# VectorE makes the last sum of probabilities, denominators before turned maxima, and the activations' loads placed anew

## The reference, cut to what matters

```python
# layer 0: 16 heads of 64, inner width 1024, no norm, all heads with own k, v
q, k, v = x @ Wq, ctx @ Wk, ctx @ Wv
logits  = q k^T / 8 + col_bias          # -20 * (1 - mask) in the columns of four tokens
out     = softmax(logits) v @ Wo + bo + x
# layers 1 to 3: 16 heads of 32, 4 heads of k and v, each shared by 4 query heads
xn  = x / sqrt(mean(x^2) + 1e-5) * norm_w
out = x + softmax((xn @ wq) k^T / sqrt(32)) v @ wo
```

## Time and profile before

| | us |
|---|---|
| median of 3 runs | 4437.71 (4436.86 to 4444.43) |
| profiled execution, its own time | 4435.94 |
| its span | 4434.0 |
| project_contexts | 0 to about 975 |
| a0 | about 975 to 2212 |
| a1 | about 2214 to 4434 |

### The profile page before, as it was taken

How to read it: one execution, slowest core, us unless ns; L and a number is a source line. 1 busy time by engine, 2 the same in 40 slices (tenths; PEclk the granted TensorE clock), 3 DMA queues, 4 the chain that set the end, 5 groups by cost and what they waited for, 6 DMA issues and landing times.

```text
span 4434.0 us, 62707 instructions
## 1 busy us (share of the span) xinstructions
PE 4157.8 (94%) x19560; PEld 2635.8 (59%) x19560; DVE 2582.5 (58%) x3586; ACT 2009.9 (45%) x2506; POOL 1842.3 (42%) x924
## 2 busy tenths in 40 slices
PE   9999999987999999999879999999999999999998
PEld 7888888874555555555535555554555544554555
DVE  3122200015556555655577777778777778777777
ACT  2111211114334333433346566656665666656665
POOL 0000000003445444544445566555665555656665
PEclk9999999998999999999979999999999999999999
DMA  5333422234444444444433322332233233322233
GB/s 183 131 128 137 160 85 82 95 108 114 121 124 114 123 122 117 118 124 124 113 83 94 87 72 78 93 105 68 75 88 94 74 85 94 87 85 75 84 88 102
DMA packets 321408, 458.07 MB, mean 103 GB/s; under 512 B 46184, under 2 KB 118888, under 8 KB 321352
## 3 DMA queue, kind: packets, MB, share of 16 engines
q1 hardware_dynamic: 321352, 457.32, 36.6%
HBM read 223.82 MB, written 102.77 MB: 74 GB/s over the span
## 4 chain that ended last, share of the span: by engine, by line
PE 36%; DVE 5%; ACT 5%; issue 4%; SPq 0%; ACTq 0%; DVEq 0%; POOL 0%; DMA 0%
PE a_ps L1186 7%; PE a_ps L1146 7%; PE a_ps L1211 6%; PE a_ps L1128 6%; PE a_ps L1170 6%; ACT a_probs L915 4%; DVE x_lo L1001 2%; PE a_ps L1197 1%; PE a_ps L1202 1%; DVE a_max_cols L995 1%; PE a_ps L1153 1%; PE a_ps L1116 0%; DVE a_qf L985 0%; DVE a_results L1036 0%; DVE wq_lo L962 0%
## 5 line engine op out<-in xcount | busy, mean ns | idle before, releaser
L995 DVE TENSOR_REDUCE a_max_cols<-a_ps 128x1 f32<-128x512 f32 x2086 | 1345.2, 677 | 298.9 <-PE a_ps L1146 294.7
L915 ACT ACTIVATE a_probs<-a_ps 128x1024 f32<-128x1024 f32 x1024 | 1016.5, 1026 | 668.9 <-PE a_ps L1170 653.5
L806 POOL TENSOR_TENSOR a_sums<-a_probs 128x1024 f32<-128x1024 f32 x256 | 606.5, 2384 | 815.9 <-ACT a_probs L915 815.9
L1146 PE MATMUL a_ps<-a_k_ops,a_q_ops 96*128 96x512 f32 x2086 | 822.6, 430 | 58.0 <-DVE a_max_cols L995 28.2
L1011 DVE RECIPROCAL a_stage<-a_stage 128x128 f32<-128x128 f32 x640 | 573.0, 925 | 491.9 <-ACT a_stage L891 491.9
L1170 PE MATMUL a_ps<-a_q_ops,a_k_ops 128*128 128x512 f32 x2560 | 789.6, 410 | 52.9 <-ACT a_probs L915 38.4
L806 POOL TENSOR_TENSOR a_sums<-a_sums,a_probs 128x1024 f32<-128x1024 f32 x320 | 768.4, 2412 | 20.7 <-POOL a_sums L806 12.7
L1186 PE MATMUL a_ps<-a_probs,a_v 128*32 128x512 f32 (+1 forms) x4096 | 662.8, 615 | 33.7 <-ACT a_probs L915 32.1
L1146 PEld LDWEIGHTS a_ps<-a_k_ops,a_q_ops 96*128 96x128 f32 x2086 | 387.9, 191 | 424.0 <-DVE a_max_cols L995 301.6
L1170 PEld LDWEIGHTS a_ps<-a_q_ops,a_k_ops 128*128 128x128 f32 x2560 | 451.4, 190 | 296.5 <-ACT a_probs L915 194.8
L881 ACT ACTIVATE a_q_ops<-a_ps 1x512 fp32r<-1x512 f32 x518 | 304.4, 588 | 296.0 <-PE a_ps L1153 289.5
(11 more groups left out here) (87 smaller groups left out, 5180.6 us busy)
## 6 DMA issues: line engine op xcount, KB each, us to landing
a_k_ops<-k_scratch SPq DMA_DIRECT2D x201, 256.0 KB, 3.9
a_q_ops<-a_qn_hi SPq DMA_DIRECT2D x792, 64.0 KB, 2.0
k_scratch<-cp_out SPq DMA_DIRECT2D x88, 512.0 KB, 2.8
a_q_ops<-a_qn_hi SPq DMA_DIRECT2D x268, 128.0 KB, 2.3
cp_raw<-in_ctx_t SPq DMA_DIRECT2D x64, 512.0 KB, 4.0
a_x_raw<-out_t SPq DMA_DIRECT2D x26, 1024.0 KB, 5.4
a_q_ops<-a_qn_lo SPq DMA_DIRECT2D x396, 64.0 KB, 2.0
a_x_res<-out_t SPq DMA_DIRECT2D x96, 256.0 KB, 3.3
```

What stands on the lines that cost most here:

```text
L806: pool.tensor_tensor(sums[:, hp], (probs if i == 1 else sums)[:, hp], probs[:, n], ALU.add)\
L915: act.activation(probs[:, s], ps[:, 2 * (s % 2):2 * (s % 2) + 2, :], ACT.Exp)\
L995: dve.tensor_reduce(max_cols[:, t % 2, col:col + 1], bank(max_bank(p)), AX.X, ALU.max, negate=True).then_inc(reduced, 1)
L1146: pe.matmul(bank(max_bank(p)), q_ops[0:SHIFT, s, h, PASS - 1, q * P:(q + 1) * P], k_ops[0:SHIFT, s, k_head(h), PASS - 1, :], start=True, s ...
```

## The change

In a0, for every tile:

- POOL makes two of the three sums; the third (`last_sum`) is made by DVE, behind its first six reductions and ahead of the reciprocals. It waits for POOL's second sum and for the fourth exponential.
- PE makes `denominators` before `turn` instead of behind it. ACT's order of `shift` and `take_denominators` stays.

In a0, for every batch: `load_x` is issued at the start of tile 4 instead of tile 0, and both rests of x are taken in tile 5 behind the sixth reduction, ahead of `last_sum`. In the last batch x of a1's first batch is loaded and split instead.

At the head of a0 v is loaded after q of tile 1; Wo goes through `x_raw` in two halves, of which only the first is loaded before the loop. They are split in batch 0, in tile 1 and tile 3, on ACT behind the third exponential and on DVE behind the fifth reduction. Each engine has an `If` for it, passed in every batch.

At the head of a1 load, rounding and rest of x fall away; PE sums the four squares itself (four matmuls instead of POOL's three adds and one matmul).

```diff
-    XAT = (1, 4)
+    WO_AT = (1, 3)
-    LOAD_AT = 2 if has_norm else 0
+    LOAD_AT = 2 if has_norm else T - 4
-        x_raw = sb("x_raw", [P, CK, S], F32)
+        x_raw = shared["x_raw"]
-            w_raw = probs[:, 0:4].rearrange("p (a b) c s -> p a (b c s)", a=2)
+            w_raw = x_raw[:, :, :].rearrange("p (a k) s -> p a (k s)", a=1)
...
             if has_norm:
-                load_x(0)
...
                 load_k(0, 0)
-                load_v(0)
-                for c in range(HALF):
-                    sp.dma_start(raw_chunk(HALF + c, c)[0], chunk(wo[0], HALF + c)).then_inc(w_in[c], DMA)
...
                 load_q(0, 0)
-                for t in range(1, AHEAD):
-                    load_k(0, t)
+                load_k(0, 1)
+                load_q(0, 1)
+                load_v(0)
+                load_k(0, 2)
+                load_q(0, 2)
+                sp.dma_start(raw_chunk(HALF, 0)[0], chunk(wo[0], HALF)).then_inc(w_in[0], DMA)
...
+                        if has_norm:
+                            x_free()
+                            load_x((it + 2) % B)
+                        else:
+                            with sp.If(it < N - 1):
+                                sp.wait_ge(w_split, HALF)
+                                x_free()
+                                load_x((it + 1) % B)
+                            with sp.Else():
+                                x_free()
+                                sp.dma_start(x_raw[:, :, :], x_out[0].rearrange("(k p) s -> p k s", p=P))\
+                                    .then_inc(x_in_s, DMA)
+                    if t == WO_AT[1] - 1 and not has_norm:
+                        with sp.If(it == 0):
+                            sp.wait_ge(w_split, 1)
+                            sp.dma_start(raw_chunk(HALF + 1, 0)[0], chunk(wo[0], HALF + 1)).then_inc(w_in[0], DMA)
...
             def sum_probs(it, t):
-                for i in range(1, max(PRE)):
+                for i in range(1, max(PRE) if has_norm else KT - 1):
...
-            if has_norm:
-                sum_squares(0)
...
             if has_norm:
-                round_x(0, 0)
                 squares(0)
...
-            if not has_norm:
-                for c in range(HALF):
-                    round_chunk(HALF + c, c, 1)
-                act.wait_ge(w_split, HALF)
...
+                        if not has_norm and t in WO_AT and s == NS // 2:
+                            with act.If(it == 0):
+                                round_chunk(HALF + WO_AT.index(t), 0, WO_AT.index(t) + 1)
...
             if has_norm:
-                split_x(0, 0)
                 rest_chunk(0, 0, 1)
...
             if not has_norm:
-                for c in range(HALF):
-                    rest_chunk(HALF + c, c, c + 1)
...
+            def last_sum(it, t):
+                dve.wait_ge(summed, (it * T + t) * SUMS + SUMS - 1)
+                dve.wait_ge(exped, (it * T + t + 1) * NS)
+                dve.tensor_tensor(sums[:, 0], sums[:, 0], probs[:, NS - 1], ALU.add).then_inc(summed, 1)
+
             def head_tile(it, t):
...
-                    if t == SPLIT_AT and i in XAT:
-                        split_x(it + 1, XAT.index(i))
+                    if t in WO_AT and i == M // 2:
+                        with dve.If(it == 0):
+                            rest_chunk(HALF + WO_AT.index(t), 0, WO_AT.index(t) + 1)
+                if t == SPLIT_AT:
+                    for c in range(XC):
+                        split_x(it + 1, c)
+                last_sum(it, t)
                 reciprocals(it, t, range(2))
...
-            def sum_squares(n):
+            def sum_squares(n, parts=1):
                 pe.wait_ge(sq_step, (n + 1) * SQ)
-                pe.matmul(bank(SUMB), ones[:, :], sq[:, 0, :], start=True, stop=True).then_inc(ssum_done, 1)
+                for k in range(parts):
+                    last = pe.matmul(bank(SUMB), ones[:, :], sq[:, k, :], start=(k == 0), stop=(k == parts - 1))
+                last.then_inc(ssum_done, 1)
...
                     outputs(it, t, kt)
+                denominators(it, t)
                 turn(*place(it, t + 1))
-                denominators(it, t)
                 free_q(it, t)
```

More of the change, by code:

```diff
@@ L702, in _ @@
                 load_v(0)
-                sp.wait_ge(x_split, 1)
-                sp.wait_ge(sq_step, 1)
+                sp.wait_ge(sq_step, SQ)
                 load_x(1)
@@ L708, in _ @@
                     .then_inc(w_in[0], DMA)
-            for t in range(0 if has_norm else 1, AHEAD):
-                load_q(0, t)
+                for t in range(AHEAD):
+                    load_q(0, t)
             with sp.Fori(0, N) as it:
@@ L718, in _, with x_free @@
                     if t == LOAD_AT:
-                        sp.wait_ge(x_split, (it + 1 + EARLIER) * XC)
-                        for i in range(RES):
-                            sp.wait_ge(stored[i], 1 + it * (UR * DMA))
-                        load_x((it + 1 + EARLIER) % B)
+                        def x_free():
+                            sp.wait_ge(x_split, (it + 1 + EARLIER) * XC)
+                            for i in range(RES):
+                                sp.wait_ge(stored[i], 1 + it * (UR * DMA))
+                        if has_norm:
[14 more added lines that the diff above has]
+                            sp.dma_start(raw_chunk(HALF + 1, 0)[0], chunk(wo[0], HALF + 1)).then_inc(w_in[0], DMA)
                     if t == 0 and has_norm:
@@ L778, in _ @@
             pool.sem_inc(added, CK)
-            if not has_norm:
-                pool.sem_inc(x_in_s, DMA)
-                pool.sem_inc(x_hi_done, XC)
-                pool.sem_inc(x_split, XC)
+            pool.sem_inc(x_in_s, DMA)
+            pool.sem_inc(x_hi_done, XC)
+            pool.sem_inc(x_split, XC)
+            if has_norm:
+                pool.sem_inc(sq_step, CK - 1)
             pool.memset(ident[:, :], 0.0).then_inc(consts, 1)
@@ L1112, in _ @@
             bank_q = q_taken if has_norm else q_lo
-            def sum_squares(n):
+            def sum_squares(n, parts=1):
                 pe.wait_ge(sq_step, (n + 1) * SQ)
-                pe.matmul(bank(SUMB), ones[:, :], sq[:, 0, :], start=True, stop=True).then_inc(ssum_done, 1)
+                for k in range(parts):
+                    last = pe.matmul(bank(SUMB), ones[:, :], sq[:, k, :], start=(k == 0), stop=(k == parts - 1))
+                last.then_inc(ssum_done, 1)
             def project_q(it, t, tiles=range(CK), first=False, early=False):
                 if t == 0 and 0 in tiles and has_norm:
-                    pe.wait_ge(ms_step, MS * it + 1)
                     if not first:
@@ L1218, in _ @@
                 pe.wait_ge(consts_v, 4)
-                sum_squares(0)
+                sum_squares(0, CK)
                 pe.wait_ge(w_split, 1)
             for t in range(AHEAD):
+                if has_norm and t == AHEAD - 1:
+                    pe.wait_ge(ms_step, 1)
                 project_q(0, t, first=(t == 0), early=True)
@@ L1387, in build @@
         project_contexts(nc, a["ctx_t"], a["wk"], a["wv"], k_scratch, v_scratch, first, bias, bias["rows"])
+        shared["x_raw"] = mem.enter_context(nc.sbuf_tensor("x_raw", [P, CK, S], F32))
         attention_layers(nc, "a0", Kind(1, INNER0, 64, False), a["x_t"], out, k_scratch, v_scratch,
```

## The result

The changed kernel takes 4453.02 us (median of 8 runs, 4449.94 to 4459.99) where the one before takes 4437.41 (median of 8, 4433.09 to 4444.43). The ratio is 1.0035, interval 1.0024 to 1.0046: slower by more than the 0.2% that can be told apart, and inside the range given. The profiled execution took 4453.12 with a span of 4451.3, so 17.3 more span than before.

What follows compares the result with a forecast made beforehand. PE, busy 94% of the span, was taken as the bound. Tile loop +17, head of a0 -13, Wo's halves +6, head of a1 -2.5 gave +7.5 on 4435.94, 4443.4; the median lies 1.8 higher: 4445, range 4410 to 4458.

Steps and rivals of the forecast that it cites:

- my own forecast: Whole kernel: the prediction's main case, 4437 to 4452 us, chance 0.45.
- Part 1: a0, third sum on DVE: stands behind `rest_output`, ends 2.30 after POOL's second sum instead of 2.50, gaining 0.2.
- the rival that DVE is first: a0: DVE's sum reaches memory before POOL's `rest_output`, outputs then bind at 15.09 a tile; 4398 us, chance 0.20.
- Part 2: a0, denominators before `turn`: reciprocals 3.54 after denominators, closing a loop of 15.86 a tile against 15.22.
- +0.64, in tiles 1 to 4, 6 and 7: a0: added time of each of these six tiles per batch, from a loop of 15.86 against 15.22.
- Part 3: a0, tile 5: both halves of x and the last sum in a row take 18.3 instead of 19.3, -1.0.
- Part 4: Head of a0: first scores at 1009.6 instead of 1022.38, -13; Wo's halves in batch 0 cost some 3 a tile, +6.
- Part 5: Head of a1: DVE's x_lo and x's load ahead of the first weights go, -2.5 (-3 to 0).
- PE's four squares end before DVE comes to them: Head of a1: PE's squares, in place of POOL's adds, finish before DVE needs them, within the -2.5.
- the rival of the small head: Head of a0: q's chain bound by SP's issues and landings, only DVE's 4.90 goes; +15.5, 4453 us, chance 0.20.
- The slack was not longer than read: Rival, a0: slack behind denominators longer, ACT's later copy costs half, +0.3 a tile for 0.64; 4429 us, chance 0.15.

Runs made afterwards that it cites:

- POOL waits: Changed kernel with POOL's `rest_output` in a0 made to wait for DVE's third sum: 4420.7 us, ratio 0.9936 to the kernel before.
- Third sum on POOL: Changed kernel with POOL making the third sum again, denominators still before `turn`: 4482.2 us, ratio 1.0066 to the kernel before.
- Turned maxima first: Changed kernel with PE's `turn` before the denominators again in a0, DVE still making the third sum: 4425.2 us, ratio 0.9941.
- Denominators copied first: Changed kernel with ACT in a0 copying the denominators before `shift`, PE's order kept: 4483.0 us, ratio 1.0061.
- Changed, filled: Changed kernel with 20 unused transposes of the identity on PE ahead of the denominators in tile 5 of a0: 4444.1 us, ratio 1.0017.
- Halves of x back: Changed kernel with the rests of x's halves behind the second and fifth reduction of tile 5 again: 4457.9 us, ratio 1.0012.
- And squares early: Changed kernel with `turn` before denominators, `rest_output` waiting for DVE's sum, and a1's four squares waiting only for the ones: 4364.7 us, ratio 0.9814.
- Heads only: Changed kernel with POOL's third sum, `turn` before denominators and x's halves back; heads, Wo's halves and later x load kept: 4448.8 us, ratio 0.9988.
- Sum only: Kernel before with two edits in a0: DVE makes the third sum and `rest_output` waits for it: 4365.7 us, ratio 0.9846.

## Why the prediction was right, and where it was off

**The number.** 4445 was forecast and 4453.0 measured: inside the range of 4410 to 4458, and 1 above the band (4437 to 4452) that my own forecast had with a chance of 0.45. By the prediction's own rule its +7.5 would have counted as no change, and +15.6 came, slower by over 0.2%, to which it gave 0.37. So the direction and the mechanisms of the tile were right, and the size was half of what came.

**The sum against the cuts.** By the prediction's own terms the four stretches would have changed by -14.2 (head, tile 0 in it), +23.3 (loop: 8 x (6 x 0.64 - 1.0) - 7 x 0.78 + 6), -2.1 (last tail and head of a1) and 0. They changed by -16.40, +33.47, -1.02 and +1.25. So the +7.5 was right in its sign and short by 10, and nearly all of it lies in the loop: +8.6 in tile 6, +3.5 for Wo's halves, +1.3 in the tails with tile 0, +1.0 in tile 5 and -4 in the other common tiles. That the total missed by no more than 10 is in part luck, since the head (-2.2) and the common tiles erred the other way.

**Part 1, right.** Predicted 2.30 from POOL's second sum to the end of DVE's, ending 1.07 after `rest_output`; the rows show 2.31 and 1.08. "POOL waits" shows it by itself, and the rival that DVE is first held in none of the common tiles. The Trainium skill (GPSIMD Engine Reference, Engine selection) would have such an add on VectorE; the durations agree (1.22 against POOL's 2.35), and once POOL waits the kernel does too. Which engine is faster at the add decided 0.2 a tile, who was first 0.8 to 0.9 (15.75 to 14.95, 15.01 to 14.08).

**Part 2, the loop right and 0.11 too long.** Loop 15.86 predicted, 15.75 measured; 3.54 from denominators to reciprocals, predicted and measured. The 0.11 lies in one term: from the load of the maxima's weights to POOL's first sum it is 2.57 (1216.84 to 1219.41), not 2.69. "Third sum on POOL" and "Turned maxima first" take the two halves of the loop apart (15.95 and 15.01), and "Denominators copied first" shows that ACT's order held it (15.4). The tail and tile 0 gave 0.60, not 0.78, a batch.

**Part 2, the step that failed:** "+0.64, in tiles 1 to 4, 6 and 7". Tile 6 got +1.71. The term was worked out at full clock, which the prediction doesn't speak of, and in six of eight batches the clock falls behind tile 5's idle. It is 8 x 1.07 = 8.6 of the 10 that are missing, and "Changed, filled" gives it back: tile 6 from 16.96 to 15.74. It could be seen in the kernel before. Three of its eight tiles 5 took 20.1 to 20.2 and the others 18.8 to 18.9, a spread that I averaged to 19.3 and didn't ask about. In one of 20.1 (1391.55 to 1411.61) the timeline has

```profile
1404.11 0.80 PE L1146 MATMUL a_ps<-a_k_ops,a_q_ops 96*128 96x512 f32 x1 [2.49 <-DVE a_max_cols L995]
```

and the granted clock stays down behind it. The first two stretches below are of that tile, the last two of the next batch's, of 18.8, in which the clock is back within the tile:

```profile
1403.00:1408.00 5.00, 3.89 (x9) 1.30 (x11) 4.34 (x6) 0.20 (x1) 4.84 (x2) 0.53 0.69 175
1408.00:1411.60 3.60, 3.60 (x14) 1.09 (x10) 0.00 (x0) 0.00 (x0) 2.17 (x2) 0.71 0.00 0
...
1552.00:1557.00 5.00, 3.98 (x11) 1.28 (x13) 4.25 (x6) 0.10 (x1) 4.84 (x2) 0.66 0.67 171
1557.00:1559.30 2.30, 2.30 (x14) 0.75 (x10) 0.00 (x0) 0.00 (x0) 2.08 (x2) 1.00 0.00 0
```

The other five common tiles took 0.10 less than predicted, -4.

**Part 3, right.** 18.3 predicted, 18.27 the median of tile 5 and 18.45 its mean. The rows show the chain as it was drawn: first rest to 1257.22, `rest_output` to 1258.36, second rest to 1259.43. (The first of these ends is 1256.15 + 1.07; its row is merged with the second's.) "Halves of x back" adds the price that Part 3 didn't have: with tile 6 counted in, the new place of the halves cost 0.76 a batch instead of gaining.

**Part 4, short on both sides.** The head gave 16.4 for 14.2, for the first scores were 15.06 earlier, not 13. Wo's halves cost 9.5 and not 6: 2.9 in tiles 1 and 3 each, as predicted, and 1.2 and 2.5 in the tiles that follow them. By all that is shown the latter are the clock's. The granted clock is 0.83 from 1035 to 1045 and 0.66 from 1071 to 1081. 1.2 is what tile 6 lost too, and the 2.5 of tile 4 is what tile 6 lost in batch 4 (18.25), where the clock is low about as long. In "And squares early" the clock stays at 1.00 behind tile 1 (1030 to 1040) and tile 2 takes 14.04, its neighbours' length; behind tile 3 it falls (0.66 from 1066 to 1071) and tile 4 takes 15.57. No run fills these two tiles. "Heads only" shows how much hangs on the neighbours: with POOL's three sums the same halves cost 14.2.

**Part 5, the sign right and the size half:** -1.3 for -2.5. "PE's four squares end before DVE comes to them" failed. I counted their matmuls and not the wait ahead of them, which the diff does not touch: for both `ones` and `k_ops`. "And squares early" gave 3.0.

**The rivals.** The head gave back more than drawn, so the rival of the small head is out, though its 4453 is the time that came: it was the right time by the wrong mechanism. The slack was not longer than read: that would have made the common tile 15.5, and it is 15.75.

## What to carry to other kernels

When work moves to the faster engine, ask whose turn it is at the memory at that moment: a DVE sum with two SBUF inputs that came 0.16 to 0.17 us behind a GpSimd operation of 1.27 waited all of it out, in 46 of 46 tiles, and one semaphore wait on the GpSimd operation that is in no hurry was worth more (0.8 to 0.9 us a tile) than the move itself (0.2). Before an instruction is moved behind the last arrival, add up its new path to the next arrival in a loop, in the other engines' written order too. And add up idle time in pieces, not in total: look at what the granted clock does behind the longest one.

## What the hardware showed that I had not expected

- TensorE's granted clock fell behind idles in one piece: 3.02 us (to 0.54 and 0.60 for some 3 us), 2.28 (0.50 and 0.68) and, in some tiles but not in others, 1.8 (0.83 over 10 us). It fell behind all eight idles of 2.49 in the kernel before and behind seven of the eight in "Sum only", but in the changed kernel not behind two of 3.32 and 3.08. It stayed at 1.00 in common tiles with pieces of some 0.5 (changed kernel) and with 1.04 ("Turned maxima first"). Filled with unused matmuls, the same stretches show 1.00. Why some idles were followed by the fall and others of the same length were not is open.
- Matmuls whose product is thrown away bought back 8 to 9 us (the idle of tile 5 in every batch) and some 27 us (an idle in every tile: the ratio went from 1.0061 to 1.0001). Tile 6 became its neighbours' length to within 0.02 in two kernels.
- Whoever came second at the port stood until the first had ended: in the changed kernel DVE's 64 adds took 1.21 to 1.23 or 2.17 to 2.19 and nothing between. POOL's `rest_output` took 1.26 to 1.29, or 2.24 to 2.26 with a rest of x ahead of it, and 1.72 and 1.73 in the two tiles in which DVE splits Wo in shorter operations.
